# A graph network on one core: column addresses computed at the head of each group of edge blocks, and gathers that don't report an index out of bounds

## The reference

```python
msg = x[src]                                        # one row per edge
agg = jax.ops.segment_sum(msg, dst, num_segments=n) # summed by destination
```

## Time and profile before

| | |
|---|---|
| time, median of 3 runs | 4643.39 us (4642.45 to 4644.51) |
| span of the profiled execution, first to last instruction | 4628.2 us |
| time of the profiled execution itself | not given beside its span; the median is 15.2 us above the span |
| busy: PE, DVE, ACT, POOL | 82%, 69%, 49%, 61% of the span |
| mean granted TensorE clock | 0.904 of full speed |

### The profile page before, as it was taken

The page is one execution under the profiler, slowest core; times in us unless marked ns, Lnnn a source line. Parts: engine busy times, 40 slices in busy tenths (PEclk is TensorE's granted clock), DMA queues, the critical chain, the costliest instruction groups (busy, mean ns, idle before and its releaser), DMA issues. The chain is left out here.

```text
span 4628.2 us, 67760 instructions
## 1 busy us (share of the span) xinstructions
PE 3772.5 (82%) x17777; PEld 2396.7 (52%) x17779; DVE 3181.4 (69%) x10005; ACT 2264.5 (49%) x4090; POOL 2802.1 (61%) x2880
## 2 busy tenths in 40 slices
PE   6797989999989999678888888876187888887876
PEld 6654556666656566444444445445144444444444
DVE  7675566554645554688888888886567777777776
ACT  6342223323232332357767765444366666666665
POOL 0174676665655500177766777773777777777774
PEclk9998999999999999888889988995588889898887
DMA  3333111121211100545555545653322222222221
GB/s 98 77 90 106 39 40 41 32 43 31 43 29 38 26 8 2 160 122 141 141 133 132 132 127 156 163 141 95 56 35 44 40 40 39 39 40 40 39 39 26
DMA packets 291738, 331.33 MB, mean 72 GB/s; under 512 B 80182, under 2 KB 246062, under 8 KB 291366
## 3 DMA queue, kind: packets, MB, share of 16 engines
q0 software_dynamic: 105328, 175.77, 18.5%
q1 hardware_dynamic: 186038, 151.23, 11.8%
HBM read 289.56 MB, written 30.77 MB: 69 GB/s over the span
## 5 line engine op out<-in xcount | busy, mean ns | idle before, releaser
L3086 POOL DMA_INDIRECT st_rows<-tabr,router_rsrc x1072 | 1028.7, 960 | 329.7 <-issue 318.8
L2438 POOL DMA_INDIRECT all_XT<-tab,graph_gsrc x880 | 852.1, 968 | 310.3 <-issue 244.2
L1446 POOL DMA_INDIRECT st_rows<-tab,graph_gsrc x748 | 741.4, 991 | 465.3 <-PE st_pe L1469 262.2
L1699 ACT ACTIVATE st_h<-st_ph,st_shift,st_scale 128x448 f32<-128x448 f32 x448 | 324.0, 723 | 729.6 <-PE st_ph L1557 729.5
L2468 PE MATMUL st_po<-all_XT,st_hot 128*128 128x264 f32 x1760 | 572.5, 462 | 36.6 <-DVE gat_sum L2659 35.3
L2659 DVE TENSOR_TENSOR gat_sum<-gat_sum,st_po 128x264 f32 x880 | 376.0, 427 | 144.8 <-DVE gat_sum L2659 97.9
L3131 PE MATMUL st_px<-all_XT,st_w 128*128 128x512 f32 (+2 forms) x832 | 427.3, 664 | 18.5 <-ACT st_hid L3191 18.5
L2468 PEld LDWEIGHTS st_po<-all_XT,st_hot 128*128 128x128 f32 x1760 | 323.4, 213 | 198.6 <-DVE gat_sum L2659 120.2
L3143 PE MATMUL st_py<-st_w,st_hid 128*128 128x256 f32 x1568 | 424.9, 418 | 0.6 <-ACT st_hid L3191 0.6
L1786 DVE TENSOR_TENSOR gcn_acc<-gcn_acc,st_pe 128x65 f32 x748 | 166.2, 222 | 348.4 <-PE st_pe L1469 257.8
L3104 PE MATMUL st_pad<-st_adr,st_hott 128*128 x1072 | 123.2, 184 | 338.6 <-DVE st_zd L3257 323.6
(11 more groups left out here) (517 smaller groups left out, 7187.1 us busy)
## 6 DMA issues: line engine op xcount, KB each, us to landing
st_bc<-drowr SPq DMA_DIRECT2D x268, 128.0 KB
st_bc<-drow SPq DMA_DIRECT2D x220, 128.0 KB
st_rows<-tabr,router_rsrc POOLq DMA_INDIRECT x1072
all_XT<-tab,graph_gsrc POOLq DMA_INDIRECT x880
st_xtb<-xtd SPq DMA_DIRECT2D x98, 128.0 KB
st_rows<-tab,graph_gsrc POOLq DMA_INDIRECT x748
tab<-gat_sum SPq DMA_DIRECT2D x7, 924.0 KB
xtd<-all_XT SPq DMA_DIRECT2D x49, 128.0 KB, 1.7
```

What stands on the lines that cost most here:

```text
L1446: g.indirect_dma_start(self.rows[:, b, u, :], None, self.R.tab0, bass.IndirectOffsetOnAxis(self.R.gsrc[:, t:t + 1], 0)).then_inc(self.s_ro ...
L1699: a.activation((self.h1, self.h2)[l][:, fb, h * HALF:(h + 1) * HALF], self.ph[:, m % 3, 0:HALF], ACT.Relu, bias=self.shift[:, l, i:i + 1], ...
L2438: g.indirect_dma_start(self.rows[:, b, u, :], None, self.R.tab1, bass.IndirectOffsetOnAxis(self.R.gsrc[:, t:t + 1], 0)).then_inc(self.s_ro ...
L3086: g.indirect_dma_start(self.rows[:, b, u, :], None, self.R.tabr, bass.IndirectOffsetOnAxis(self.R.rsrc[:, t:t + 1], 0)).then_inc(self.s_ro ...
```

## The change

Two things. First, two helpers are added, and every edge stage computes its four addresses with them right behind the load of the window numbers, at the head of the group; the adds (and the score matmuls) then use registers that are ready. In Prelude and Stage1 this also puts the load and the address computation ahead of the one-hot, where they stood behind it. Second, the `indirect_dma_start` of each of the four edge stages is issued with `oob_is_err=False`. [...] No index here is out of bounds. The gathers of L679 and L2027 keep the flag. In the diff, the hunk of Prelude's gathers stands for Stage1, Stage2 (`tab1`) and Stage3 (`tabr`, `rsrc`) too, that of Stage2's scores and loop for Stage3 (`adr`, `R.racc`) too; `add` takes the addresses in place of the numbers.

```diff
+def placed(engine, aps):
+
+    for ap in aps:
+        engine.lower_ap(ap)
+    return aps
+
+
+def columns_of(tile, ws):
+
+    return [tile[:, bass.ds(w, 1), :].rearrange("p a d -> p (a d)") for w in ws]
...
@@ Prelude.pool @@
                 g.indirect_dma_start(self.rows[:, b, u, :], None, self.R.tab0,
-                                     bass.IndirectOffsetOnAxis(self.R.gsrc[:, t:t + 1], 0)).then_inc(self.s_rows[b], 16)
+                                     bass.IndirectOffsetOnAxis(self.R.gsrc[:, t:t + 1], 0), oob_is_err=False).then_inc(self.s_rows[b], 16)
...
@@ Prelude.vector @@
         def add_edges(q):
+            aws = placed(v, columns_of(acc, self.windows(ENG.DVE, q)))
             one_hot(q + self.HOTS - 1)
-            ws = self.windows(ENG.DVE, q)
             v.wait_ge(self.s_sum, q + 1)
-            for u in range(GROUP):
+            for u, aw in enumerate(aws):
                 if GROUP * q + u:
                     v.wait_ge(self.s_acc, GROUP * q + u)
-                aw = acc[:, bass.ds(ws[u], 1), :].rearrange("p a d -> p (a d)")
                 v.tensor_tensor(aw, aw, self.pe[:, q % 2, u * GCOL:(u + 1) * GCOL], ALU.add).then_inc(self.s_acc, 1)
...
@@ Stage1.vector @@
             for q in qs:
-                one_hot(q + self.HOTS - 1)
                 t = GROUP * (self.first() + q)
                 _, ws = self.nc.values_load_multi_w_load_instructions(
                     R.gwin[0:1, t:t + GROUP], engines=(ENG.DVE,), min_val=0, max_val=W - 1,
                     skip_runtime_bounds_check_because="a count of at most W - 1 windows")
+                aws = placed(v, columns_of(self.acc, ws))
+                one_hot(q + self.HOTS - 1)
                 v.wait_ge(self.s_sum, q + 1)
...
@@ Stage2.tensor @@
-            ws = self.windows(ENG.PE, q)
+            near = placed(t, [self.adl[:, bass.ds(w, 1), :, :].rearrange("p a k h -> p (a k h)")
+                              for w in self.windows(ENG.PE, q)])
             t.wait_ge(self.s_tt, q + 1)
...
             for u in range(GROUP):
-                mm = t.matmul(self.pad[:, u].rearrange("p k h -> p (k h)"), self.hott[:, q % self.HOTT, u],
-                              self.adl[:, bass.ds(ws[u], 1), :, :].rearrange("p a k h -> p (a k h)"),
+                mm = t.matmul(self.pad[:, u].rearrange("p k h -> p (k h)"), self.hott[:, q % self.HOTT, u], near[u],
                               start=(u == 0), stop=False, skip_group_check=True)
...
@@ Stage2.vector @@
         for q in range(self.GROUPS):
             n, b = divmod(q, self.STEP)
-            ws = self.windows(ENG.DVE, q)
+            aws = placed(v, columns_of(R.gat, self.windows(ENG.DVE, q)))
             exponents(q + 2)
             one_hot(q + 5)
-            add(q, ws)
+            add(q, aws)
             message(q + 2)
```

More of the change, by code:

```diff
@@ L1780, in add_edges @@
                     skip_runtime_bounds_check_because="a count of at most W - 1 windows")
+                aws = placed(v, columns_of(self.acc, ws))
+                one_hot(q + self.HOTS - 1)
                 v.wait_ge(self.s_sum, q + 1)
-                for u in range(GROUP):
+                for u, aw in enumerate(aws):
                     if GROUP * q + u:
                         v.wait_ge(self.s_acc, GROUP * q + u)
-                    aw = self.acc[:, bass.ds(ws[u], 1), :].rearrange("p a d -> p (a d)")
                     v.tensor_tensor(aw, aw, self.pe[:, q % 2, u * GCOL:(u + 1) * GCOL], ALU.add).then_inc(self.s_acc, 1)
@@ L2651, in message, with add @@
                 .then_inc(self.s_msg, 1)
-        def add(q, ws):
-            for u in range(GROUP):
+        def add(q, aws):
+            for u, aw in enumerate(aws):
                 v.wait_ge(self.s_sum, GROUP * q + u + 1)
@@ L2657, in add @@
                     v.wait_ge(self.s_acc, GROUP * q + u)
-                aw = R.gat[:, bass.ds(ws[u], 1), :].rearrange("p a d -> p (a d)")
                 v.tensor_tensor(aw, aw, self.po[:, (GROUP * q + u) % self.BANKS, 0:GROW], ALU.add).then_inc(self.s_acc, 1)
@@ L3086, in pool @@
                 g.indirect_dma_start(self.rows[:, b, u, :], None, self.R.tabr,
-                                     bass.IndirectOffsetOnAxis(self.R.rsrc[:, t:t + 1], 0)).then_inc(self.s_rows[b], 16)
+                                     bass.IndirectOffsetOnAxis(self.R.rsrc[:, t:t + 1], 0), oob_is_err=False).then_inc(self.s_rows[b], 16)
     def tensor(self, t):
@@ L3096, in scores @@
                 return
-            ws = self.windows(ENG.PE, q)
+            near = placed(t, [self.adr[:, bass.ds(w, 1), :, :].rearrange("p a k h -> p (a k h)")
+                              for w in self.windows(ENG.PE, q)])
             t.wait_ge(self.s_tt, q + 1)
@@ L3103, in scores @@
             for u in range(GROUP):
-                mm = t.matmul(self.pad[:, u].rearrange("p k h -> p (k h)"), self.hott[:, q % self.HOTT, u],
-                              self.adr[:, bass.ds(ws[u], 1), :, :].rearrange("p a k h -> p (a k h)"),
+                mm = t.matmul(self.pad[:, u].rearrange("p k h -> p (k h)"), self.hott[:, q % self.HOTT, u], near[u],
                               start=(u == 0), stop=False, skip_group_check=True)
@@ L3284, in message, with add @@
             v.tensor_tensor(part[:, :, 2, :], rows, part[:, :, 1, :], ALU.subtract).then_inc(self.s_part, 1)
-        def add(q, ws):
+        def add(q, aws):
             v.wait_ge(self.s_sum, q + 1)
             n = PARTS * FROW
-            for u in range(GROUP):
+            for u, aw in enumerate(aws):
                 if GROUP * q + u:
                     v.wait_ge(self.s_acc, GROUP * q + u)
-                aw = R.racc[:, bass.ds(ws[u], 1), :].rearrange("p a d -> p (a d)")
                 v.tensor_tensor(aw, aw, self.po[:, q % self.SUMB, u * n:(u + 1) * n], ALU.add).then_inc(self.s_acc, 1)
@@ L3422, in vector @@
         for q in range(self.GROUPS):
-            ws = self.windows(ENG.DVE, q)
+            aws = placed(v, columns_of(R.racc, self.windows(ENG.DVE, q)))
             exponents(q + 2)
             one_hot(q + 5)
-            add(q, ws)
+            add(q, aws)
             for u in range(len(self.judged)):
```

## The result

The changed kernel takes 4601.49 us (median of 4 runs, 4598.20 to 4603.88) against 4643.95 us before: a ratio of 0.9909 with a 95% interval of 0.9896 to 0.9922, so 42 us less (36 to 48). The forecast was 4620, 23 us less: the sign and the range held, the size was little more than half of what came.

What follows compares the result with a forecast made beforehand. POOL's gathers bound Prelude, Stage3 and most of Stage2, where DVE's pace held POOL 42 us; PE bounds Stage1. Stage2 -25, Prelude +2, rest 0: -23 us on 4643.4 gives 4620, range 4601 to 4634 (0.50).

Steps and rivals of the forecast that it cites:

- The register instruction between the adds: DVE's adds: each register instruction between them costs 0.105 us; three of four adds gain it, 0.94 us per round of three groups.
- The head: Start of each group on DVE: forming four addresses there, joined in pairs, costs 0.25 us.
- Rivals 1 and 3: Rival 1: nothing moves, 4634 to 4653 us (0.20). Rival 3: the bare head decides, slower, 4664 us at H = 0.6 (0.10).
- What of it is bare: Stage2's heads on DVE: nothing behind the message, 0.25 us behind `variance`, 0.20 behind `weigh_values`: 0.45 per round of three groups.
- Stage2's gain: DVE's pace falls from 5.40 to 5.24 us per group, so POOL's true waits fall from 42 to 17 us: gain 25.
- Stage1: PE's stage; PE waits for DVE's adds only 7.8 us, so between -5 and +5 us, taken as 0.
- Stage3: POOL's stage, not held by DVE: the same DVE edits change 0 us, within 2 us in the drain.
- Prelude: Head moved past the one-hot costs 0.18 us per group, 6 us if all counts; partly hidden by waits for ACT: +2 us.
- PE's scores: PE's register instructions move ahead of the waits; PE isn't the pace in Stage2 or Stage3: 0 us.
- the flag: Gathers without the out-of-bounds error report: between -0.185 and +0.185 us each, taken as 0.
- Rivals 2 and 4: Rival 2: gathers get shorter, 17 us off per 10 ns (0.12). Rival 4: gathers get longer, 10 ns more leave 4637 us (0.08).
- a head that costs nothing: Stage2 case at the fast end of the forecast: buffers never full, gain 42 us, the most there is; 4601 us.

Runs made afterwards that it cites:

- Stage2's adds: Kernel before, with only the addresses of DVE's adds in Stage2 formed at the group's head: 4615.26 against 4645.14 us, ratio 0.9936.
- the pair of traces: Kernel before with only the gathers' flag changed (4643.72 us), beside the changed kernel with the flag back, so only addresses changed (4601.37 us).
- the run of it alone: Kernel before, with only Stage1's edit (addresses at the head, one-hot behind them): 4628.77 against 4641.02 us, ratio 0.9975.
- three other runs with the same Stage3: Changed kernel with Stage2's adds undone (4630.79 us), with Stage1's one-hot first again (4597.84), or with Stage2's head issued behind the message of the group before (4582.42).
- the flag alone: Kernel before, with only `oob_is_err=False` set on the gathers of the four edge stages: 4643.72 against 4645.14 us, ratio 0.9996.

## Why the prediction was right, and where its size was off

- *The register instruction between the adds, 0.105 each:* right (0.21 to 0.10).
- *The head, 0.25:* right to 0.01, though one pair takes 93 ns and not 75. Two start 0.124 apart: handing over costs 0.03, less than I took. Rivals 1 and 3 end here. The issue floor that the Trainium skill gives in Runtime: NRT & Kernel Launch (Instruction fetch mechanics), taken as the price of one register instruction, would have made both small; the step from 0.30 to 0.55 us behind `variance` and the 30 us of Stage2's adds speak against it as a price. A floor as such they don't contradict.
- *What of it is bare, 0.45 per round:* 0.25 + 0.11 = 0.36, since the multiply covers more. DVE's pace came to 5.21, not 5.24.
- *Stage2's gain, 25:* 32, by two terms. Its gathers got 27.6 us shorter from first to last (1160.4 to 1132.8), near the forecast of 25: POOL's true waits fell from 40 us in this trace to 10, not 17, while the gathers themselves took 2 us more. The other 4.6 I left out: I priced only POOL's waits, but the stage ends with DVE's last add, and DVE's lag behind the last gather fell from 16.5 to 11.9.
- *Stage1, 0 (-5 to 5):* the step that failed, -17 in the pair of traces and -12 (-7 to -16) in the run of it alone, of which 8 to 9 are PE's waits, and the rest goes with the granted clock. I took PE's wait for the adds, 7.8 us, as all that DVE's adds can cost PE. It is the one wait that did not move. The adds stand in one queue with the norms and sums of the tokens, and PE waits for those 36 us more.
- *Stage3, 0:* the second miss, hidden by the first: +10 in its gathers (+5 in three other runs with the same Stage3), -4 in the drain. I had argued that POOL isn't held by DVE because no wait says so the earlier trace rows. A collision makes no wait; it makes the instruction longer.
- *Prelude, +2:* 0, 205.9 us from its first gather to Stage1's in both traces. *PE's scores, the flag:* 0, right: Stage2 takes 1146 us with the scores changed and the adds not, and Stage3's gathers 1355. Rivals 2 and 4 are out by the flag alone.

Sum by the traces: -17 + 2 - 32 + 10 - 4 = -41, against -25 + 2. The 2 of the first sum lie between Stage1's last add and Stage2's first gather; the 2 of the second were Prelude's, which lost nothing.

Two things were luck. The median of 4601.49 is the end of the forecast that stood for a head that costs nothing (4601), yet the head costs 0.25: Stage1, which was put at 0, and the 7 us more of Stage2 brought 24 us, of which Stage3 took 6 back. And that end was itself summed without Prelude's 2 us: by the prediction's own terms the forecast went from 4603 (-42 + 2) to 4637 (-8 + 2), not from 4601 to 4634.

## What to carry to other kernels

A register computation between dependent instructions costs its full 0.1 us each time; move it under a long instruction, and look at where exactly it lands: directly behind a 1.2 us message it was free, behind a chain of 0.17 us steps it cost 0.25 per round of three, 13 us of Stage2. Where PE waits for an engine, add up its waits for everything in that engine's queue, not for the instruction that you shorten. And where POOL's gathers set the pace, compare their mean with their median before and after: a step that shifts DVE's two-input instructions against the gathers costs without any wait to show it.

## What the runs showed of the hardware

A gather that starts within the first 0.29 us of a 128x512 bf16 `tensor_tensor` with both operands in SBUF is mostly held until some 0.29 us into it, up to 0.26 us more (0.94 to 1.20). In a row of sixteen 0.48 us `scalar_tensor_tensor` of that kind one gather was held to the end of the row (4.19 us), and another, which started 0.01 us after one of them, not at all (0.94). Of 1072 gathers 71 to 105 met a one-hot in the runs with Stage3's addresses at the head and 48 to 55 in the two without that are listed above, which is some 5 to 11 us more. Why the addresses at the head move the one-hots towards the gathers' starts is open: it wasn't tried to move the one-hot by itself. The same program's Stage1 took 1170 us in one execution and 1180 in another, which is most of the 15 us between the span that the forecast began with and the median. PE's waits were 84 us in both; its busy time was 1086 and 1096, at a granted clock of 0.98 and 0.97. Why the clock differed, the runs don't tell.
